# Edge network of a graph kernel: who adds a group's sums into the accumulator, and who scales the heads

## The reference, cut to what matters

```
for h in range(4):                                       # four heads, D = 64 each
    alpha = concat([q_i * K_v[src], q_i * K_E], 1) * scale      # q_i = K_v[dst]
    gate  = sigmoid(_ln(alpha, ln_g[h], ln_b[h]))               # layer norm over 128
    m = concat([V_v[src], V_E], 1)
    m = (m @ Wu[h] + bu[h]) * gate
    m = leaky(_ln(m @ Wm[h] + bm[h], mln_g[h], mln_b[h]))       # layer norm over 64
    heads.append(segment_sum(m, dst, num_segments=6250))
out = concat(heads, 1) @ Wc + bc
```

## Time and profile before

| what | value |
|---|---|
| median of three runs | 13212.4 us (13209.07 to 13218.26) |
| the profiled execution's own time | 13231.73 us, its span 13229.9 us |
| busy share of the span: PE, PEld, DVE, ACT, POOL | 70%, 46%, 67%, 44%, 67% |
| the sweep's product (line 682), first and last of 404 | 4158.4 and 11230.6 us |
| granted TensorE clock, mean | 0.93 |

### The profile page before, as it was taken

One profiled execution on the slowest core, in us unless ns is written; L12 is line 12 of the kernel. 1 busy time (PEld: TensorE's weight loads), 2 busy tenths in 40 slices (PEclk: granted clock), 3 DMA queues, 4 the chain that ended last, 5 costly groups with the idle time before them and its releaser, 6 DMA issues.

```text
span 13229.9 us, 180603 instructions
## 1 busy us (share of the span) xinstructions
PE 9252.9 (70%) x45190; PEld 6129.7 (46%) x45190; DVE 8863.8 (67%) x20382; ACT 5824.9 (44%) x11467; POOL 8813.8 (67%) x6219
## 2 busy tenths in 40 slices
PE   1344444444475888888888888888888888669997
PEld 0233333333223665666666665666666656323322
DVE  3233333333206888888888888888888888327896
ACT  0111111111102666666666666666666666006442
POOL 1588888888603888888888888888888888000000
PEclk9999999999997999989999899999999999889997
DMA  9766666666693443434343344344443343569663
GB/s 413 235 157 150 151 152 151 150 152 153 163 416 109 120 119 119 120 119 120 119 120 119 118 120 120 119 120 119 119 120 120 119 119 110 231 279 359 232 219 125
DMA packets 1232544, 2147.28 MB, mean 162 GB/s; under 512 B 345985, under 2 KB 768210, under 8 KB 1218579
## 3 DMA queue, kind: packets, MB, share of 16 engines
q1 hardware_dynamic: 838120, 1657.69, 36.7%
q0 software_dynamic: 390240, 484.27, 16.9%
q10 hardware_dynamic: 4048, 3.51, 0.1%
HBM read 1652.11 MB, written 492.84 MB: 162 GB/s over the span
## 4 chain that ended last, share of the span: by engine, by line
POOL 44%; issue 20%; PE 15%; DMA 8%; DVE 5%; ACT 3%; SPq 3%; POOLq 1%; DVEq 1%; another core or an unknown queue 0%; ACTq 0%; PEldq 0%
POOL arena L1362 22%; POOL adj L1401 14%; POOL arena L1414 6%; PE psum L1273 5%; DMA arena<-adj 4%; DMA adj<-put_val,put_idx 3%; SPq L1453 3%; PE psum L1318 2%; ACT arena L980 2%; POOL arena L1417 1%; PE psum L1131 1%; PE psum L1285 1%; PE psum L1196 1%; PE psum L1209 1%; PE psum L1186 1%
## 5 line engine op out<-in xcount | busy, mean ns | idle before, releaser
L1401 POOL DMA_INDIRECT adj<-put_val,put_idx x1616 | 2638.3, 1633 | 844.9 <-issue 478.1
L980 ACT ACTIVATE arena<-arena 128x128 f32<-128x128 f32 x6464 | 2657.6, 488 | 298.2 <-DVE arena L774 170.4
L1110 PE MATMUL psum<-ke,arena 64*128 64x256 f32 x3232 | 1451.8, 640 | 1883.2 <-DMA arena<-in_edge_t 1883.2
L1362 POOL DMA_INDIRECT arena<-table1q,idx_dst x1616 | 2249.3, 1392 | 492.6 <-issue 492.6
L1362 POOL DMA_INDIRECT arena<-table,idx_blk x1616 | 1903.5, 1178 | 431.5 <-issue 374.9
L1110 PEld LDWEIGHTS psum<-ke,arena 64*128 64x128 f32 x3232 | 1039.7, 329 | 2294.9 <-issue 2025.9
L1196 PEld LDWEIGHTS psum<-wm,arena 128*128 128x128 f32 x12928 | 1755.6, 203 | 608.0 <-issue 509.4
L986 ACT ACTIVATE arena<-psum,cols 128x512 f32<-128x512 f32 x1616 | 1250.0, 774 | 1710.8 <-PE psum L1178 1386.7
L1186 PE MATMUL psum<-arena,wvu 128*128 128x512 f32 x3232 | 1894.1, 671 | 83.0 <-DVE arena L703 60.2
L1209 PE MATMUL psum<-arena 128*128 128x128 f32 x6464 | 1113.3, 325 | 1119.7 <-DVE arena L730 1107.0
L1196 PE MATMUL psum<-wm,arena 128*128 128x64 f32 x12928 | 1798.2, 285 | 5.9 <-issue 4.6
(11 more groups left out here) (208 smaller groups left out, 11727.7 us busy)
## 6 DMA issues: line engine op xcount, KB each, us to landing
arena<-adj SPq DMA_DIRECT2D x192, 1568.0 KB, 12.5
arena<-adj SPq DMA_DIRECT2D x336, 896.0 KB, 4.7
kept_keys<-arena SPq DMA_DIRECT2D x404, 512.0 KB
arena<-kept_keys SPq DMA_DIRECT2D x404, 512.0 KB
adj<-arena SPq DMA_DIRECT2D x98, 1568.0 KB
arena<-in_edge_t SPq DMA_DIRECT2D x808, 128.0 KB
kept_hot<-arena SPq DMA_DIRECT2D x404, 256.0 KB
arena<-kept_hot SPq DMA_DIRECT2D x404, 256.0 KB
```

The lines of the kernel that those rows point to most:

```text
L980: A.activation(to, at_, ACT.Identity, bias=shift[z][:, n:n + 1], scale=rstd[z][:, n:n + 1]).then_inc(normed, 1)
L1110: last = M.matmul(psum[:, 2 + 2 * z + j, t * H * D:(t + 1) * H * D], edge0[z][:, 2 * j + t, :], ke[D:P, :], start=True, stop=True)
L1362: K.indirect_dma_start(out=dst[:, t, :], out_offset=None, in_=table, in_offset=bass.IndirectOffsetOnAxis(ap=idx[:, t:t + 1], axis=0)).then ...
L1401: K.indirect_dma_start(out=adj, out_offset=bass.IndirectOffsetOnAxis(ap=put_idx[s][:, j:j + 1], axis=0), in_=put_val[s][:, j:j + 1], in_of ...
```

## The change

ScalarE takes the sums of a whole group out of PSUM; VectorE no longer adds them. For this TensorE accumulates all four tiles of a group into one window of 512 nodes (two PSUM banks, 0 and 1), at a column offset for each tile that it reads from registers (`offs`, the distance of a tile's first node to the group's first). It clears the two banks with zero matmuls first. ScalarE adds the window's first column to what is in `acc` (that node may have begun in the group before) and copies the other 511 columns over. GpSimd's multiplication by `mg` goes away; VectorE does scale by deviation and by norm weight in one instruction for each of the 16 pairs of tile and head. The turned x moves from bank 0 to bank 7, and the bias matmul of `o_pair` comes first and covers both tiles.

```diff
-NW = NP + WIN
+NW = NP + G * WIN
-        bm_parts = sb("bm_parts", [3, H * D], BF16)
+        zero_row = sb("zero_row", [1, P], BF16)
+        bm_parts = sb("bm_parts", [3, 2 * H * D], BF16)
...
+        offs = rel[0:1, :].bitcast(I32)
-        C2 = 1
+        C2 = G * H
...
-        def block_bases(engine, g):
-            return bases(engine, dst_t[0:1, bass.ds(g * G, U * G)])
+        def group_bases(engine, g):
+            first = dst_t[0:1, bass.ds(g * G, U * G)].rearrange("p (u t) -> p u t", t=G)[:, :, 0]
+            return bases(engine, first)
+
+        def block_offsets(engine, g):
+            _, regs = nc.values_load_multi_w_load_instructions(
+                offs[0:1, bass.ds(g * G, U * G)], engines=(engine,), min_val=0, max_val=(G - 1) * WIN, ...)
+            return regs
...
 # VectorE
+            link(V.tensor_tensor(offs..., dst_t..., first node of each group..., ALU.subtract))
-                if now[4] and s == 0:
-                    held[:] = block_bases(DVE, i - 4)
-                regs = held[G * s:G * s + G]
-                def add(t): ... V.tensor_tensor(at_, at_, sums, ALU.add).then_inc(added1, 1)
-                    dve.wait_ge(y_affine, 2 * (i - 3))
+                    dve.wait_ge(y_affine, i - 3)
...
                 if now[3]:
-                    V.tensor_tensor(y[odd], o_sb[odd], root[:, Q:2 * Q].unsqueeze(2).to_broadcast([P, Q, D]),
-                                    ALU.mult).then_inc(chain2, 1)
-                add(0)
-                add(1)
+                    for n in range(Q):
+                        h = n % H
+                        V.scalar_tensor_tensor(y[odd][:, n, :], o_sb[odd][:, n, :], root[:, Q + n:Q + n + 1],
+                                               mg[:, h * D:(h + 1) * D], ALU.mult, ALU.mult).then_inc(chain2, 1)
                 if now[1]:
                     gate_m(3)
-                add(2)
-                add(3)
...
 # ScalarE, at the start and the end of an iteration
+                if now[4] and s == 0:
+                    held[:] = group_bases(ACTE, i - 4)
...
                     take_o(1)
+                if now[4]:
+                    act.wait_ge(sums1, 2 * (i - 3))
+                    after(act, added1, 3 * (i - 4))
+                    for half in range(2):
+                        own = acc[:, half, bass.ds(held[s], 1)]
+                        A.activation(own, psum[:, half, 0:1], ACT.Identity, bias=own).then_inc(added1, 1)
+                    A.activation(acc[:, :, 1:NW][:, :, bass.ds(held[s], G * WIN - 1)], psum[:, 0:2, 1:G * WIN],
+                                 ACT.Copy).then_inc(added1, 1)
...
 # TensorE
+                if now[4] and s == 0:
+                    held[:] = block_offsets(PE, i - 4)
...
                 def o_pair(j):
-                    pe.wait_ge(gm_ready, H * (i - 1))
                     after(pe, o_taken, 2 * (i - 2) + j)
+                    M.matmul(psum[:, 6, :], ones3[:, :], bm_parts[:, :], start=True, stop=False)
+                    pe.wait_ge(gm_ready, H * (i - 1))
                     for t in range(2):
                         for h in range(H):
-                            M.matmul(..., wm[:, h, :], start=h == 0, stop=False)
-                        last = M.matmul(psum[:, 6, at_:at_ + H * D], ones3[:, :], bm_parts[:, :],
-                                        start=False, stop=True)
+                            last = M.matmul(..., wm[:, h, :], start=False, stop=t * H + h == 2 * H - 1)
+
+                def clear_sums():
+                    after(pe, added1, 3 * (i - 4))
+                    for half in range(2):
+                        M.matmul(psum[:, half, :], zero_row[0:1, :], zero_row[0:1, 0:1].to_broadcast([1, G * WIN]),
+                                 start=True, stop=False)
 
                 def sums(j):
-                    after(pe, added1, G * (i - 5) + 2 * j + 2)
...
-                            last = M.matmul(psum[:, 1 + 6 * j, at_:at_ + WIN], <message>,
-                                            onehot[z][:, t, :], start=True, stop=True)
+                            last = M.matmul(psum[:, half, bass.ds(held[G * s + t], WIN)], <message>,
+                                            onehot[z][:, t, :], start=False, stop=t == G - 1)
...
                 if now[4]:
+                    clear_sums()
                     sums(0)
...
 # GpSimd
                 pool.wait_ge(chain2, C2 * (g + 1))
-                K.tensor_tensor(y4, y4, mg[:, :].unsqueeze(1).to_broadcast([P, G, H * D]),
-                                ALU.mult).then_inc(y_affine, 1)
-                pool.wait_ge(y_affine, 2 * g + 1)
                 K.tensor_tensor(y4, y4, mb[:, :].unsqueeze(1).to_broadcast([P, G, H * D]),
                                 ALU.add).then_inc(y_affine, 1)
```

More of the change, by code:

```diff
@@ L25 @@
 PE = mybir.EngineType.PE
+ACTE = mybir.EngineType.Activation
 P = 128
@@ L141, in gnn @@
         vecs = sb("vecs", [D, 6])
[L142 to L144 removed]
+        bm_row, bm_rest, bm_up = (acc[0:1, i // 2, NP + i % 2 * H * D:NP + (i % 2 + 1) * H * D].rearrange(
+            "p (h d) -> p h d", h=H) for i in range(3))
+        zero_row = sb("zero_row", [1, P], BF16)
         bm_part = [sb(f"bm_part{i}", [1, H * D], BF16) for i in range(3)]
[L146 removed]
+        bm_parts = sb("bm_parts", [3, 2 * H * D], BF16)
         ones3 = sb("ones3", [3, P], BF16)
@@ L417, in halves_of @@
             return slice(half * HALF + i * CH_N, half * HALF + (i + 1) * CH_N)
-        def block_bases(engine, g):
-            return bases(engine, dst_t[0:1, bass.ds(g * G, U * G)])
+        def group_bases(engine, g):
[3 more added lines that the diff above has]
+            _, regs = nc.values_load_multi_w_load_instructions(
+                offs[0:1, bass.ds(g * G, U * G)], engines=(engine,), min_val=0, max_val=(G - 1) * WIN,
+                skip_runtime_bounds_check_because="every node has an edge, so a tile begins at most a window on")
+            return regs
         @block.vector
@@ L498, in _ @@
             link(V.memset(ones3[:, :], 1.0))
+            link(V.memset(zero_row[:, :], 0.0))
             dve.wait_ge(s_iota, 4)
@@ L943, in _ @@
             for i in range(3):
-                A.dma_start(bm_parts[i:i + 1, :], bm_part[i][:, :]).then_inc(bm_in, 16)
+                for t in range(2):
+                    A.dma_start(bm_parts[i:i + 1, t * H * D:(t + 1) * H * D], bm_part[i][:, :]).then_inc(bm_in, 16)
             dve_done(f"key_turn{len(TC) - 1}")
@@ L969, in sweep1 @@
             def sweep1(i, k, s, inside):
-                now = [inside or 0 <= i - lag < NG for lag in range(3)]
+                now = [inside or 0 <= i - lag < NG for lag in range(5)]
                 z, odd = s % 2, (s + 1) % 2
+                if now[4] and s == 0:
+                    held[:] = group_bases(ACTE, i - 4)
                 def norm(g, slot, z, h):
@@ L1018, in sweep1 @@
                     take_o(1)
-            steps(act, sweep1, NG, 4, 2)
+                if now[4]:
[6 more added lines that the diff above has]
+                                 ACT.Copy).then_inc(added1, 1)
+            held = []
+            steps(act, sweep1, NG, 8, 4)
             for i in range(NBLK):
@@ L1170, in turn_x @@
                     for t in range(G):
-                        last = M.transpose(psum[0:D, 0, t * P:(t + 1) * P], pair[s][:, t, 0:D], ident[:, :])
+                        last = M.transpose(psum[0:D, 7, t * P:(t + 1) * P], pair[s][:, t, 0:D], ident[:, :])
                     last.then_inc(xt_turned, 1)
@@ L1195, in o_pair @@
                         for h in range(H):
-                            M.matmul(psum[:, 6, at_ + h * D:at_ + (h + 1) * D], gm[z][:, h, 2 * j + t, :],
-                                     wm[:, h, :], start=h == 0, stop=False)
-                        last = M.matmul(psum[:, 6, at_:at_ + H * D], ones3[:, :], bm_parts[:, :],
-                                        start=False, stop=True)
+                            last = M.matmul(psum[:, 6, at_ + h * D:at_ + (h + 1) * D], gm[z][:, h, 2 * j + t, :],
+                                            wm[:, h, :], start=False, stop=t * H + h == 2 * H - 1)
                     last.then_inc(o_done, 1)
+                def clear_sums():
[3 more added lines that the diff above has]
+                                 start=True, stop=False)
                 def sums(j):
@@ L1204, in sums @@
                     pe.wait_ge(msg_ready, i - 3)
-                    after(pe, added1, G * (i - 5) + 2 * j + 2)
                     for t in (2 * j, 2 * j + 1):
                         for half in range(2):
-                            at_ = (t % 2 * 2 + half) * WIN
-                            last = M.matmul(psum[:, 1 + 6 * j, at_:at_ + WIN],
+                            last = M.matmul(psum[:, half, bass.ds(held[G * s + t], WIN)],
                                             msg[z][:, t * H + 2 * half:t * H + 2 * half + 2, :].rearrange("p h d -> p (h d)"),
```

(2 more changed lines are left out.)

27 lines of the change are left out of this document (11 added, 16 removed).

## The result

The changed kernel takes 13,091.92 us (median of four runs, 13,046.31 to 13,101.9) against 13,215.0 of the kernel before (four runs): the ratio is 0.9901, 95% interval 0.9885 to 0.9917. I had forecast 12,772 us, 443 us less; 123 us came. The measured time lies 2 us outside of my range. The direction was right, the size was not.

What follows compares the result with a forecast made beforehand. GpSimd bounds at 17.55 us a group; VectorE would then bound at 16.3: 1.25 us gained, 0.15 given back, -1.10 x 403 = -443, +3 outside the sweep, -440 us, giving 12,772 us. Its own range was 12,640 to 12,900.

Steps and rivals of the forecast that it cites:

- The bound before: GpSimd bounds the edge sweep at 17.55 us a group; without its `mg` pass (2.46 us) its floor is 15.09.
- The 16 scalings: VectorE's new y instructions: 0.286 us each, 0.20 apart, 3.2 us for 16 (2.3 to 4.6).
- VectorE at 16.3 us: VectorE's work per group after the change, 13.10 + 3.2 us, making it the new bound above GpSimd's 15.1.
- ScalarE's three instructions: Two one-column additions and one 2x511 copy between `take_o(1)` and the norm of head 1: 1.5 us (0.9 to 2.0).
- TensorE's work: TensorE's load per group with zero matmuls, register loads and steps: 15.8 us, 17.0 with both upper ends, against VectorE's 16.3.
- allowance of 0.15 us a group: Time given back for iterations in which TensorE or ScalarE makes VectorE wait; bounds 0 and 0.6 us.
- my own sign of being wrong: One stated sign: gates wait for ScalarE's sigmoids or TensorE's m by more than 0.6 us a group.
- now shrink: TensorE's idle gaps, behind which it sometimes ran at 1.2 GHz (0.91 of its clock granted), were to get smaller.
- the cover: Slack between sigmoid 1's end on ScalarE and `gate_m(1)` needing it: 0.7 us (0.2 to 1.3).
- TensorE becomes the bound: Rival: unhidden register steps and clears make TensorE's path 17.1 us a group, about 13,035 us; 14%.
- slower rival: Two rivals: VectorE's short chain isn't overlapped, about 13,270 us, 6%; the chain shuts GpSimd's gathers out, about 13,515, 6%.

Runs made afterwards that it cites:

- e4: The changed kernel plus 12 filler transposes per group (result unused) on TensorE, ahead of its wait for the norm of head 1: 12,711.9 us.
- e2: The changed kernel with y in one VectorE instruction and the multiplication by `mg` back on GpSimd, so only the accumulator half: 13,176.3 us.
- e1: The changed kernel with ScalarE taking a group's sums one iteration later, behind sigmoid 1: 13,018.7 us.
- e7: The changed kernel plus e4's 12 filler transposes, and y in two instructions of 128x1024 in place of 16 of 128x64: 12,689.4 us.
- e9: e7 plus 70 one-column clears of an unused column ahead of VectorE's sweep loop, shifting the loop's place in its program: 12,400.0 us.

## Why the prediction was wrong, point by point

- **The bound before** was GpSimd, and its floor fell as priced. GpSimd now waits 290.2 / 117 = 2.5 us a group for y, which leaves 14.7 us for itself; in e4 it is 16.26 - 141.0 / 123 = 15.1, the forecast's figure.
- **The 16 scalings** are 0.277 us each (forecast 0.286) and take 7054.48 - 7051.32 = 3.16 us (forecast 3.2). The rule of the Trainium skill that I weighed ("VectorE: DVE Perf Modes", "The DRAIN you can't avoid") would have given 4.6, taken as I took it; the trace does not agree, instructions start 0.20 us apart. I had left out the section's last remark, that an instruction which isn't held starts earlier, and these rows are in keeping with that.
- **VectorE at 16.3 us** is what an undisturbed group takes (16.28), and with the clock held up every group (16.26 in e4).
- **ScalarE's three instructions** take 7073.82 - 7072.62 = 1.20 us (forecast 1.5). But loading its four registers cost nearly as much as VectorE's sixteen in the kernel before, not a quarter: the load took 0.89 us against 1.10.
- **TensorE's work** was put too high, 15.8 us a group: it was busy for 1724.54 / 117 = 14.7 and idle for (204.8 + 55.0 + 15.6) / 117 = 2.35. So it isn't the amount of its work that makes it late.
- **The step that failed is the allowance of 0.15 us a group** "for iterations in which TensorE or ScalarE makes VectorE wait after all (bounds 0 and 0.6)". It measured 17.16 - 16.26 = 0.90 us, 363 us over the sweep, against 60 allowed. These 303 us are nearly all of the 320 between forecast and result. It is also past the upper bound, and my own sign of being wrong came: gates waiting for sigmoids by more than 0.6 us a group, measured 0.76. I had written that the idle gaps "now shrink" and had taken the clock to rise with that. TensorE's idle time did shrink, from (2000 - 1631.52) / 114 = 3.2 to 2.35 us a group; but 204.8 us of it now lie ahead of the turn of head 1, where it waits for the norm, and in the kernel before only this:

```profile
PE psum L1178 <- ACT arena L980: 28.4, 27, 1.1
```

The granted clock fell from 0.91 to 0.89, in 41 stretches instead of 87, of up to 14 us instead of 7. And I had worked out the cover (0.7 us for sigmoid 1) from one group, in which the granted clock was 1.00 throughout. A low stretch delays `o_pair(1)` and the sums, and behind those ScalarE now stood with three more instructions. The row that could have warned me was at hand: in the kernel before ScalarE's sigmoids waited for TensorE by up to 5.3 us, and yet VectorE waited at no gate. The likely reason is that GpSimd's slower round left room, as e2 bears out, where gate waits of up to 4.9 us cost nothing; and that room is what the change removed.
- **Rivals.** "TensorE becomes the bound" came nearest in time (13,035), but for another reason: in e4, with clears and register steps in place and the clock at 1.00, VectorE waits for nothing. Neither slower rival appeared. Of the changed kernel's gathers in the sweep, the 258 that began under one of the 16 scalings took 0.97 us at most, as short as those under nothing; the 296 that began under the product took 2.83 us (median), as the earlier trace rows had it. The rule on exclusive access in the Trainium skill ("SBUF — State Buffer", "Who interferes with whom") agrees with the long ones, and with the short ones as far as each short instruction lets a gather in.

Not settled: why the low stretches of the changed kernel last longer, why there are more of them with the adds later (59, all of 10 us or more, in e1), why twelve fillers hold the clock and five don't, and what about a loop's place makes its code be fetched again.

## What to carry to other kernels

When the bound moves to an engine, work out each cover twice, with TensorE's rows at 2.4 and at 1.2 GHz; waits that were free beside a slower engine can cost time afterwards. A mean over groups hides this: compare the undisturbed group with the disturbed one before naming a cause. And when a variant misses by a few microseconds once per loop pass, look at the instruction queue's bytes before blaming the edit.

## What the runs showed of the hardware that I had not expected

- Work without use on TensorE made the kernel 2.9% faster (e4 against the changed kernel, 12,711.9 and 13,091.9 us), by the clock: 0.89 to 1.00.
- The place of VectorE's loop in its program was worth about 2.2% (e7 and e9, ratios 0.9604 and 0.9393): 4.41 MB against 0.43 MB of instructions fetched, 3.0 against 0.3 us behind each branch. The Trainium skill ("Advanced Engine Details and Errata", section "ISA Cache") gives VectorE's sequencer two cache lines; that a loop's fit depends on where it starts is in keeping with e9, and no run here tests it further.
- Two passes of 128x1024 cost VectorE less than 16 fused ones of 128x64: 15.51 us a group in e9 against 16.26 in e4, both at a granted clock of 1.00.
- A chain of 16 short VectorE instructions doesn't delay GpSimd's gathers (0.97 us at most), one of 128x2048 does (2.83 us).
